# First scan of a four-layer kernel: POOL waits for the first stage's low part before its four operations on the drive

## The reference

```
dq = q - q ** 3 / 3.0 - p + drive + tanh(q) @ coupling.T + bias
dp = EPSILON * (q + ALPHA - BETA * p)
dq1, dp1 = f(q, p)
dq2, dp2 = f(q + 0.5 * DT * dq1, p + 0.5 * DT * dp1)
dq3, dp3 = f(q + 0.5 * DT * dq2, p + 0.5 * DT * dp2)
dq4, dp4 = f(q + DT * dq3, p + DT * dp3)
q_next = clip(q + DT / 6.0 * (dq1 + 2 * dq2 + 2 * dq3 + dq4), -20, 20)
p_next = clip(p + DT / 6.0 * (dp1 + 2 * dp2 + 2 * dp3 + dp4), -20, 20)
```

## Time and profile before

| | |
|---|---|
| median of 3 runs | 1920.07 us (1919.12 to 1921.48) |
| the profiled execution | 1918.98 us |
| its span, from first to last instruction | 1917.3 us |
| mean granted clock of PE | 0.754 |
| DVE busy | 1353.7 us, 71% of the span |
| PE busy | 1402.8 us, 73% of the span |
| POOL busy | 615.3 us, 32% of the span |
| stretch from the scan's first POOL operation to its last step's | 258.1 to 906.6 us |

### The profile page before, as it was taken

One profiled execution on the slowest core, in us unless ns is written; L12 is line 12 of the kernel. 1 busy time (PEld: TensorE's weight loads), 2 busy tenths in 40 slices (PEclk: granted clock), 3 DMA queues, 4 the chain that ended last, 5 costly groups with the idle time before them and its releaser, 6 DMA issues. The chain is left out here.

```text
span 1917.3 us, 48177 instructions
## 1 busy us (share of the span) xinstructions
PE 1402.8 (73%) x16570; PEld 1093.4 (57%) x16570; DVE 1353.7 (71%) x6930; ACT 711.6 (37%) x2888; POOL 615.3 (32%) x1605
## 2 busy tenths in 40 slices
PE   6898855555555555555389999999998388989865
PEld 4476633333333333333178888888886166767654
DVE  4357779999999999999565555556554746565654
ACT  4658722222222222222434343334333543434322
POOL 1035535555555555555221111111111712121110
PEclk9979975555555555555689999999999688788855
DMA  3000000000000000000210100000002100000000
GB/s 117 0 1 2 2 1 2 2 2 2 2 2 2 2 2 2 2 2 2 93 50 1 34 18 6 29 17 1 1 1 81 41 1 3 2 3 14 3 14 24
DMA packets 15084, 28.05 MB, mean 15 GB/s; under 512 B 1692, under 2 KB 9464, under 8 KB 14584
## 3 DMA queue, kind: packets, MB, share of 16 engines
q1 hardware_dynamic: 14672, 24.93, 3.8%
q10 hardware_dynamic: 168, 0.04, 0.0%
HBM read 20.77 MB, written 4.19 MB: 13 GB/s over the span
## 5 line engine op out<-in xcount | busy, mean ns | idle before, releaser
L795 PE MATMUL bank<-s_tanh_hi,coup_hi 128*128 128x16 f16 x2048 | 141.5, 179 | 318.8 <-ACT s_tanh_hi L786 318.8
L795 PEld LDWEIGHTS bank<-s_tanh_hi,coup_hi 128*128 128x128 f16 x2048 | 95.0, 108 | 366.1 <-ACT s_tanh_hi L786 366.1
L786 ACT ACTIVATE s_tanh_hi<-s_s 128x32 f16<-128x32 f32 x384 | 88.0, 229 | 358.0 <-DVE s_s L662 358.0
L1221 POOL TENSOR_TENSOR prob<-prob,inv 128x512 f32<-128x512 f32 x64 | 66.5, 1040 | 426.7 <-DVE inv L1187 426.7
L1107 ACT ACTIVATE prob<-bank,neg_max 128x128 f32<-128x128 f32 x256 | 90.5, 366 | 215.6 <-DVE neg_max L1156 215.6
L795 PE MATMUL bank<-s_tanh_lo,coup_hi 128*128 128x16 f16 x2048 | 140.8, 179 | 9.2 <-DVE s_tanh_lo L656 0.6
L1694 POOL TENSOR_TENSOR stage_area<-x,h 128x32 f32<-128x32 f32 x128 | 45.8, 358 | 295.6 <-DVE h_lo L1636 294.0
L795 PE MATMUL bank<-s_tanh_hi,coup_lo 128*128 128x16 f16 x2048 | 130.0, 174 | 0.0
L997 PE MATMUL bank<-x_hi,w_hi 128*128 128x512 f32 x256 | 111.4, 435 | 22.9 <-DVE w_lo L1136 21.2
L795 PEld LDWEIGHTS bank<-s_tanh_lo,coup_hi 128*128 128x128 f16 x2048 | 94.2, 107 | 48.2 <-DVE s_tanh_lo L656 13.0
L1415 PE MATMUL bank<-h_hi,w_h_hi 128*128 128x16 f16 x1536 | 92.7, 173 | 30.0 <-DVE h_hi L1629 30.0
(11 more groups left out here) (286 smaller groups left out, 4561.5 us busy)
## 6 DMA issues: line engine op xcount, KB each, us to landing
w_stage<-in_L_cond_qkv_w_dram SPq DMA_DIRECT2D x12, 512.0 KB, 5.0
x_tok<-in_x_dram SPq DMA_DIRECT2D x4, 512.0 KB, 5.6
ow_stage<-in_L_cond_out_w_dram SPq DMA_DIRECT2D x4, 512.0 KB, 5.7
x_in<-x SPq DMA_DIRECT2D x1, 2048.0 KB, 11.7
stage_area<-in_L_cond_ffn_w_dram SPq DMA_DIRECT2D x2, 1024.0 KB, 6.9
keep_area<-x_in SPq DMA_DIRECT2D x1, 2048.0 KB, 12.6
out_dram<-stage_area SPq DMA_DIRECT2D x64, 32.0 KB, 1.6
ada_w<-in_L_cond_ada_w_dram SPq DMA_DIRECT2D x1, 1536.0 KB, 12.3
```

What stands on the lines that cost most here:

```text
L786: A.activation(th_hi[:, :], s, ACT.Tanh).then_inc(hi_ready, 1)
L795: ins = nc.tensor.matmul(coupled[:, B * m:B * m + B], w[:, o:o + P], th[:, B * c:B * c + B], start=(first and c == 0 and m == 0), stop=(la ...
L1221: G.tensor_tensor(prob[:, grp % 2, :, :], prob[:, grp % 2, :, :], inv[:, grp % 2, :].unsqueeze(2).broadcast_to([P, HG, T]), MUL).then_inc( ...
```

## The change

One line is added. In each step j POOL now waits, ahead of its four operations on the drive, until `lo_ready` has reached 4 j + 1, that is until DVE has finished `low(1)` of this very step. Nothing else differs; the lines behind it are numbered one higher in the changed kernel.

```diff
                 if j:
                     pool.wait_ge(dve_done, ND * j - 1)
+                pool.wait_ge(lo_ready, 4 * j + 1)
                 do(G.tensor_tensor(qd1, gh, q, ADD))
                 do(G.tensor_tensor(qd2, qd1, gh, ADD), False)
                 do(G.tensor_tensor(gmq, gh, q, SUB))
```

## The result

| | before | changed |
|---|---|---|
| median | 1919.14 us (7 runs, 1916.14 to 1921.48) | 1926.35 us (7 runs, 1923.09 to 1934.75) |
| profiled execution | 1918.98 us | 1934.75 us |
| starts of `qd1`, first and last step | 258.1, 906.6 | 260.5, 921.8 |
| one step, from these over 127 | 5.106 us | 5.207 us |

The ratio is 1.0038, with a 95% interval of 1.0028 to 1.0049: the changed kernel is slower by 7.2 us, where I had forecast 4.2 us of gain. It lies 4.8 us above the upper end of the range. The profiled execution is the longest of the seven and shows more of the loss than the median has: 0.101 us a step, 12.8 of its 15.8 us.

What follows compares the result with a forecast made beforehand. Bound: one chain through all four stages of a step. Terms -0.06 + 0.01 - 0.035 + 0.055 = -0.03 us a step, times 128 -4.2 us, forecast 1915.9 us; range 1909.5 to 1921.5.

Steps and rivals of the forecast that it cites:

- First stage, gain: Stage one: `qd1` no longer lies ahead of `cube`, which takes 0.18 instead of 0.245 us; 0.06 us gained a step.
- Where POOL goes: POOL's queue: `qd1` starts 0.43 us later, L769 0.35 us later, `mscaled` at 808.06 to 808.14 us.
- Second stage: Stage two: `gmq` can hold the square or `m2`, `base3` is freed; 0.01 us of loss, bounds -0.015 to +0.03.
- the edge of harm: DVE against POOL: a two-input operation starting within about 0.11 us behind POOL's two-tensor operation is held.
- the wake-up: Head of POOL's queue: `qd1` starts 0.08 us after the low part of stage one ends.
- Third stage: Stage three: L772 moves behind the low part, which it had lengthened to 0.22 us; 0.035 us of gain.
- Fourth stage: Stage four: `mscaled` starts right ahead of a DVE operation before the low part and holds it; 0.055 us of loss.
- The fourth rival: Stages two, three and four: POOL holds DVE ahead of the low part, up to 0.11 us each; slower, chance 0.13.

Runs made afterwards that it cites:

- the low part alone: Changed kernel without the wait for `trace`, so POOL waits for the low part of stage one only; 1923.26 us against 1920.64 before, ratio 1.0014.
- the swapped waits: Changed kernel with the wait for `lo_ready` written first and the one for `dve_done` behind it; 1923.32 us against 1920.71 before, ratio 1.0018.
- The kernel with `psum` behind `m3s`: Changed kernel with POOL waiting for `base1` instead, and `psum` put behind `m3s` on POOL; 1917.46 us against 1920.71 before, ratio 0.9983.
- `base1`: Changed kernel with POOL's two waits replaced by one for this DVE operation; 1913.75 us against 1920.64 before, ratio 0.9958.

## Why the prediction was wrong

*First stage, gain: right.* `cube` went from 245 to 184 ns, stage one from 1.33 to 1.27 us, as forecast.

*Where POOL goes: 0.07 us too early, and then 0.12 and 0.13 us too late.* I took 0.08 us from the end of the low part to `qd1`, from a row in which the operation had one wait. With two it was 0.15 us (812.16 to 812.31). POOL's rows of the changed kernel, quoted with the change, show two waits on it, and I had priced the second at nothing; the low part alone and the swapped waits show that it decides. Further down I let L769 start 0.08 us behind the end of `gmq3`, as if it had to wait; with its wait long met it starts 0.04 us ahead of that end (813.23 + 0.34 against 813.53). From L769 to `mscaled` I took the 1.89 us of before; it was 1.76 (813.53, 815.29). So the delay of POOL, 0.50 us at `qd1`, had shrunk to 0.14 at `mscaled`, where I had 0.28 to 0.35.

*Second stage: the step that failed.* I forecast 0.01 us of loss with a bound of 0.03; it was 0.15 (1.38 against 1.23). I asked of `base2` only whether `qd1` would be there in time, and never set it against `qd2`'s start. By my own schedule these were 0.13 us apart (805.21, and 805.40 less 0.06), just outside the edge of harm, and the 0.07 us of the wait put them on each other. And I bounded the loss by one hold less the 0.05 us for which DVE waits for tanh. Two holds in a row add 0.09 and 0.10 us and have that slack only once. The kernel without `gmq` gives the split: with `base2`'s hold alone stage two is 1.25 us.

The two kernels in which `qd1` does stand at 0.69 us, where I had put it, show what the rest of the working was worth: they lose 2.6 us. So the wake-up accounts for some 4.6 of the 11.4 us between forecast and result, and the holds in stages two and three, which I had as 0.01 us of loss and 0.035 of gain, would have made the forecast's sign wrong without it.

*Third stage: wrong sign.* I forecast 0.035 us of gain; it was 0.05 of loss. `psum` did not leave the low part but came closer to its start, 0.04 us ahead instead of 0.08, since against `trace` it had come 0.14 us later and the low part 0.10.

*Fourth stage: no loss in this step.* `mscaled` starts 0.07 us behind `advance` (815.22, 815.29), just as before. `psum` holds the low part of stage three in both kernels, and `advance` starts 0.67 us behind `psum` in both (807.04 and 807.71, 814.55 and 815.22), `mscaled` 0.74: held by `psum`, DVE had become late together with POOL. In the 30 steps in which the square was free, the loss that I forecast is there: `mscaled` 0.29 us behind `advance`, `m4` at 0.24 us, and stage four 0.06 us longer, where I had 0.055. The kernel with `psum` behind `m3s` shows such a loss too.

Together for this step: -0.06 + 0.15 + 0.05 + 0 = +0.14 us. The mean over the steps is 0.10, since in those 30 steps, with -0.07, +0.06, -0.02 and +0.06, it is 0.03. The fourth rival was the nearest: holds in three stages that exceed 0.093 us. Its places are those of the trace, the one in stage four in 30 steps alone, and I gave it 0.13. What I should have done is to lay the whole of POOL's new schedule beside DVE's, start by start: with 0.07 us between them, `qd1` at 0.69 and at 0.76 us differ by a whole hold.

The Trainium skill, "SBUF — State Buffer", section "Who interferes with whom", says that issue order decides who blocks. The trace agrees for these two: `qd1`, started 0.01 us behind `p2` in the changed kernel, itself took 0.29 us (812.31), and `qd2`, started 0.03 us ahead of `base2`, took 0.25 and made DVE take 0.27. At 0.013 us the order of the starts that the profile shows doesn't settle it: the square, that much behind `gmq`, was lengthened in 93 steps, and `gmq` in 30.

## What to carry to other kernels

When an operation of one engine is delayed to free another, its successors move too: write down the new starts of all of them against the other engine's, and don't stop at the place that was freed. A loss hidden by slack can be hidden once; add up the holds in a stage before subtracting the slack. And look at more than one step: here two kinds of step differ by 0.11 us with the same starts. Try the wait at several places (here for `base1`, `cube`, the low part, `m1`: -6.9, -4.2, +2.6, +13.7 us), and if an operation has two waits, write first the one that will be met last: here that order was 4.6 us better.

## What the runs showed of the hardware

How long a DVE operation of two SBUF inputs is held falls with its distance behind the start of a POOL operation of two tensors. Undisturbed it takes 0.18 us. In all rows of the table POOL's operation took its undisturbed 0.25 or 0.26 us.

| pair | kernel | distance, us | DVE's operation, us |
|---|---|---|---|
| `gmq`, square | changed | 0.01 | 0.28 |
| `qd2`, `base2` | changed | 0.03 | 0.27 |
| `gmq`, square | low part alone | 0.03 | 0.27 |
| `qd1`, `m1` | `base1` | 0.04 | 0.26 |
| `qd1`, `cube` | before | 0.07 | 0.24 |
| `gmq`, `base2` | `base1` | 0.08 | 0.22 |
| `qd2`, `base2` | low part alone | 0.12 | 0.18 |

Distance and lengthening add up to 0.11 to 0.13 us: DVE is let go about that long behind POOL's start, not at its end 0.25 us behind it. Where POOL's own operation was lengthened first, to about 0.3 us, the hold reaches further: before, `rest` started 0.10 us behind `qd2` (0.29 us) and still took 0.24, and in the changed kernel `m4` took 0.24 at 0.11 us behind `mscaled` (0.30 us).

`advance`, which reads PSUM, was not lengthened by a POOL operation: in the kernel that waits for `cube` it starts 0.08 us behind `qd2` and takes the usual 0.25 us. What I hadn't expected is the wait: the same two conditions put the operation's start at 0.69 us when the one met last is written first, and at 0.76 when it is written last.
